# Unread products, a shared PSUM bank and a later start of heads and shared expert in the streamed stage of a transformer kernel

## The reference

```python
x = x + L0_attn(layernorm(x))       # ends in  a @ Wo + bo
x = x + L0_ffn(layernorm(x))        # router, routed experts, shared expert
x = x + L1_attn(layernorm(x))       # w_q_b, w_kv_b and w_o, 16 heads
x = x + L1_ffn(layernorm(x))

# in L0_ffn:
scores = softmax(x @ w_router.T); topw, topi = top_k(scores, 6)
routed = sum over the chosen experts of  topw * (silu(x @ g) * (x @ v) @ o)
out = routed + silu(x @ swg) * (x @ swv) @ swo
# in L1_attn:
w_o_abs = einsum('rhd,hde->hre', w_uv, w_o3)
q_abs   = einsum('bshd,rhd->bshr', q_nope, w_uk)
```

## Time and profile before

| | us |
|---|---|
| median of 3 runs | 2289.82 |
| lowest and highest | 2288.16, 2292.33 |
| the profiled execution, its time | 2300.19 |
| the profiled execution, its span | 2298.7 |
| the changed stage in the trace | 603 to 819 |
| idle of GpSimd before scatters, waiting for slots | 77.0 |

### The profile page before, as it was taken

One profiled execution on the slowest core, in us unless ns is written; L12 is line 12 of the kernel. 1 busy time (PEld: TensorE's weight loads), 2 busy tenths in 40 slices (PEclk: granted clock), 3 DMA queues, 4 the chain that ended last, 5 costly groups with the idle time before them and its releaser, 6 DMA issues. The chain is left out here.

```text
span 2298.7 us, 41540 instructions
## 1 busy us (share of the span) xinstructions
PE 1993.8 (87%) x11702; PEld 1336.9 (58%) x11766; DVE 1451.2 (63%) x3115; ACT 1256.6 (55%) x2558; POOL 882.9 (38%) x899
## 2 busy tenths in 40 slices
PE   4987999999767679999648899999698999996698
PEld 1552333333345469999624577777545777775587
DVE  4887888888355579999257566665265555543443
ACT  0793777777533147777114577777144777771322
POOL 1340000000054647797053277777001666670100
PEclk7896999999967889999869899999898999998899
DMA  7953000000531259898321012112000111012000
GB/s 210 289 104 56 2 0 0 1 0 1 126 118 59 83 168 267 263 287 266 106 69 41 10 45 53 42 42 56 14 0 1 24 24 35 21 35 68 1 19 19
DMA packets 185938, 173.83 MB, mean 76 GB/s; under 512 B 19651, under 2 KB 170741, under 8 KB 184822
## 3 DMA queue, kind: packets, MB, share of 16 engines
q1 hardware_dynamic: 173750, 143.23, 22.6%
q0 software_dynamic: 10720, 29.44, 3.9%
q10 hardware_dynamic: 1376, 0.02, 0.0%
HBM read 96.15 MB, written 61.60 MB: 69 GB/s over the span
## 5 line engine op out<-in xcount | busy, mean ns | idle before, releaser
L2638 POOL TENSOR_TENSOR w_rest<-work,w_head 128x512 fp32r<-128x512 f32 (+3 forms) x384 | 395.4, 1041 | 224.9 <-ACT w_head L2595 222.6
L790 DVE TENSOR_REDUCE half_max<-m_ps 128x1 f32<-128x512 f32 x512 | 317.2, 683 | 58.2 <-PE m_ps L712 57.6
L2484 DVE TENSOR_REDUCE piece_max<-m_ps 128x1 f32<-128x512 f32 (+3 forms) x384 | 201.1, 549 | 205.9 <-PE m_ps L2411 161.7
L847 ACT ACTIVATE weights<-s_ps 128x512 f32<-128x512 f32 x512 | 266.2, 601 | 108.2 <-PE s_ps L730 108.2
L2591 ACT ACTIVATE work<-s_ps 128x512 f32<-128x512 f32 (+3 forms) x384 | 187.4, 488 | 103.0 <-PE s_ps L2439 79.0
L2595 ACT ACTIVATE w_head<-work 128x512 fp32r<-128x512 f32 (+3 forms) x384 | 201.3, 524 | 56.9 <-PE o_ps L2448 46.7
L712 PE MATMUL m_ps<-kT,qT 96*128 (+1 forms) x512 | 204.3, 400 | 8.5 <-DVE half_max L790 6.6
L730 PE MATMUL s_ps<-qT,kT 99*128 (+1 forms) x512 | 193.3, 384 | 9.5 <-DMA qT<-max_rows 5.1
L2448 PE MATMUL o_ps<-w_head,lat_head 128*128 128x512 f32 (+3 forms) x384 | 184.4, 480 | 1.4 <-POOL w_rest L2638 1.4
L887 POOL COPY v_now<-v 128x83 f32 (+1 forms) x64 | 16.0, 256 | 366.6 <-PE o_ps L742 361.7
L1095 POOL TENSOR_TENSOR gv_rest<-ex_wgv,gv_head 128x736 fp32r<-128x736 f32 x64 | 113.9, 1779 | 75.8 <-ACT gv_head L1192 75.8
(11 more groups left out here) (395 smaller groups left out, 5050.8 us busy)
## 6 DMA issues: line engine op xcount, KB each, us to landing
slots<-zero SPq DMA_DIRECT2D x8, 3456.0 KB, 27.5
rows<-slots SPq DMA_DIRECT2D x64, 256.0 KB, 3.4
slots<-ex_out SPq DMA_DIRECT2D x64, 256.0 KB, 3.0
ex_wgv<-in_L_ffn_wg_dram SPq DMA_DIRECT2D x72, 176.0 KB, 3.0
ex_wgv<-in_L_ffn_wv_dram SPq DMA_DIRECT2D x72, 176.0 KB, 3.3
ex_wo<-in_L_ffn_wo_dram SPq DMA_DIRECT2D x72, 128.0 KB, 3.2
oT<-work SPq DMA_DIRECT2D x64, 128.0 KB
w_down<-l_inverse SPq DMA_DIRECT2D x32, 256.0 KB
```

The lines of the kernel that those rows point to most:

```text
L790: dve.tensor_reduce(half_max[:, u:u + 1], m_ps[:, BANK[u], :], AX.X, ALU.max).then_inc(max_done, 1)
L847: act.activation(w[:, s % 2 * 4 + j, :], s_ps[:, BANK[4 * s + j], :], ACT.Exp, scale=HD ** -0.5).then_inc(w_done, 1)
L2484: dve.tensor_reduce(piece_max[:, qt, k0 // 512:k0 // 512 + 1], m_ps[:, r % 2, 0:n], AX.X, ALU.max).then_inc(d["max_done"], 1)
L2638: pool.tensor_tensor(w_rest[:, s % 3, c0:512], w[:, s % 3, c0:512], w_head[:, s % 3, c0:512], ALU.subtract).then_inc(d["w_rest_done"], 1)
```

## The change

It has four parts. `keep_busy(n)` issues n matmuls of 128 x 512 in bf16 (identity by identity) into a bank of its own, `busy_ps`, which nobody reads; they wait for nothing and signal nothing. They stand before every `head` (2 before the second head of a pair, which is computed at the start of the next step, 1 before the first), before `shared_up` (1), before `ranks` (2), before `shared_down` (1), and 16 once before the first `turn_head`: 88 in all. The bank is won by putting the logits into the unused half of `x_ps`. For that, `logit(t)` waits until ScalarE has copied the turned rows of tile t + 1 in place of tile t, and `turn_x(t)` waits for the copy of the logits of tile t - 2. HEADS_AT goes from 6 to 7 and CHUNKS_AT from 14 to 15, on all engines, and STEPS with it from 23 to 24.

```diff
-    HEADS_AT, CHUNKS_AT = 6, 14
+    HEADS_AT, CHUNKS_AT = 7, 15
     STEPS = CHUNKS_AT + T // 2 + 1
...
-        l_ps = l.ps("l_ps", [P, 512])
+        busy_ps = l.ps("busy_ps", [P, 512])
...
+        l_ps = x_ps[:, D:D + NE]
...
+                def keep_busy(n):
+
+                    for _ in range(n):
+                        pe.matmul(busy_ps[:, :].rearrange("p (a b) -> p a b", a=4), c.identb[:, :],
+                                  c.identb[:, :].unsqueeze(1).to_broadcast([P, 4, P]), start=True, stop=True)
...
                 def turn_x(t):
                     pe.wait_ge(d["xn_done"], t + 1)
                     reuse(pe, d["x_copied"], t, 1)
+                    reuse(pe, d["log_copied"], t, 2)
...
-                    pe.wait_ge(d["x_copied"], t + 1)
+                    pe.wait_ge(d["x_copied"], min(t + 2, T))
                     reuse(pe, d["log_copied"], t, 1)
...
                     if 0 < h <= H1:
+                        keep_busy(2)
                         head(h - 1)
                     if 0 <= n < T // 2:
+                        keep_busy(1)
                         shared_up(n)
                     if 0 <= s - 2 < T:
                         turn_x(s - 2)
...
+                    if h == 0:
+                        keep_busy(16)
                     if 0 <= h < H1:
                         turn_head(h)
                     if 0 <= s - 3 < T:
                         logit(s - 3)
                     if 0 <= h < H1:
+                        keep_busy(1)
                         head(h)
                     if 0 <= s - 4 < T:
+                        keep_busy(2)
                         ranks(s - 4)
                     if 0 <= h < H1:
                         turn_head(h + 1)
                     if n > 0:
+                        keep_busy(1)
                         shared_down(n - 1, 0)
                         shared_down(n - 1, 1)
```

More of the change, by code:

```diff
@@ L1604, in logit @@
                         pe.wait_ge(d["wr_copied"], 1)
-                    pe.wait_ge(d["x_copied"], t + 1)
+                    pe.wait_ge(d["x_copied"], min(t + 2, T))
                     reuse(pe, d["log_copied"], t, 1)
                     for k in range(DK):
-                        i = pe.matmul(l_ps[:, 0:NE], xT[:, k, t * P:(t + 1) * P], w_r[:, k, :], start=k == 0,
+                        i = pe.matmul(l_ps, xT[:, k, t * P:(t + 1) * P], w_r[:, k, :], start=k == 0,
                                       stop=k == DK - 1)
@@ L1727, in copy_logits @@
                     act.wait_ge(d["log_done"], t + 1)
-                    act.activation(logits[:, t, :], l_ps[:, 0:NE], ACT.Copy).then_inc(d["log_copied"], 1)
+                    act.activation(logits[:, t, :], l_ps, ACT.Copy).then_inc(d["log_copied"], 1)
                 def deviation(t):
```

## The result

Over 20 runs of each, the changed kernel has a median of 2297.42 us (2290.67 to 2307.27) and the kernel before 2291.28 us (2282.01 to 2303.25): a ratio of 1.0027 with a 95% interval of [1.0015, 1.0039]. The change makes the kernel some 6 us slower, 3 to 9. The forecast was 6.6 us faster, and 2297.42 lies just outside the range's upper end of 2297.0.

A forecast was written before the change was run, and what follows sets the result against it. The streamed stage was taken as a chain round TensorE, ScalarE and VectorE per token tile, GpSimd's scatters at its end. Terms -4.5 - 6.1 + 3 + 1 = -6.6 us took 2289.82 to 2283.2 us, range 2268 to 2297.

The forecast's parts named there:

- The move: Heads and shared expert one step later: last slot earlier; -4.5 us, the middle of 0.75 and 8.25 us gain.
- The bank: Logits in the turned rows' bank wait for ScalarE's copy, 0.9 us in three shared steps, mostly covered: +1 us.
- The clock: Heads' stretch: products raise TensorE's mean clock from 0.74 to about 0.87; half of 16.3 us, times busy share: -6.1 us.
- given back: Rival: clock rises, but late signals stay and the gain becomes "remote" idle; 2289 us (2286 to 2292), chance 0.22.
- The products: The 88 unread matmuls on TensorE, mostly covered by idle time, leave some open before ranks and in shared steps: +3 us.
- The sixteen: Products before the first turned head, 3.7 to 6.9 us inside a 10.5 us wait for loads: costed at nothing.
- The slower rival: Clock in the heads' stretch stays at 0.74 or below, each product 0.43 us: +11 us, 2301 us, chance 0.16.
- Carrying the profile over: Whole kernel: the 10.4 us by which the median lay below the profiled execution was carried over unchanged.

The follow-up runs named there:

- e4: The changed kernel without its 88 unread products, move and shared bank kept: ratio 0.9992 to the kernel before, median 2288.21 us.
- e8: The changed kernel with unread products tripled everywhere but the sixteen, 232 in all: ratio 1.0057 to the kernel before, median 2307.90 us.
- e17: The changed kernel without the sixteen products before the first turned head, the other 72 kept: ratio 1.0002 to the kernel before, median 2295.47 us.
- e9: The changed kernel with only the sixteen products before the first turned head, move and bank kept: ratio 0.9987 to the kernel before, median 2294.71 us.
- e7: The changed kernel with each 512-column product cut into eight of 64 columns: ratio 1.0055 to the kernel before, median 2306.89 us.
- e1: The kernel before with only heads and shared expert moved by one step: ratio 0.9976 to the kernel before, median 2288.97 us.
- e16: The changed kernel with products cut into eighths and one scatter per tile in place of six: ratio 0.9772 to the kernel before, median 2237.77 us.

## Why the prediction was wrong

**The move (-4.5).** Right by itself: -5.5 [-8.9, -1.8]. The ranks of step 6 start at 630.63 in the changed kernel, before 636. But the last scatter came at 800.53, only 1.8 us before 802.33, with the first turned head 3.2 us earlier (638.87 against 642.11 in the earlier trace rows): in the changed kernel the gain of the move was spent before the last slot.

**The bank (+1).** Its run gives -0.7 [-4.6, 3.2]; the term is within it and too small to be told.

**The clock (-6.1).** This is the step that failed. The excess of cold time was there and a good part of it went (118.66 to about 102 us of other work, some 17, where I had 16.3 in the heads' stretch and 5.3 in the shared one as the most), though the mean in the heads' stretch came to 0.77 and not to 0.87. I then took TensorE's busy share, 68.85/92.1, as the share in which it is waited for. Beside the scatters the saved time did not reach the end of the stage (177.3 us in the changed kernel, 160.2 in e4, 174.6 in the kernel before): in the longest waits TensorE's results were there, and ScalarE took them up later (13.1 us in the longest case, 87.8 us of late waits in place of 77.7). The busy share did not measure who is waited for. This is the mechanism of the rival *given back*, and the sign that I gave for it, grown "remote" idle, is there (77.7 to 87.8 us); but I had put its end at 2289 us, since I let it only take the gain and not add to the loss. Between e4 and e8 the clock rose from 0.78 to 0.89 and the kernel became 15 us slower by the ratios. The Trainium skill, "TensorE: Matmul & The Clock Gate", section "Terms", reckons the penalty as the throttled time by one minus the clock's share; no such gain shows in these runs, but since each of them also added products, they don't test that rule by itself.

**The products (+3).** This term failed with it: the runs measure clock and products only together. Cover by idle time was the argument; the products did lie in the idle time, and the idle time before the heads still grew from 16.8 to 21.8 us. With signals on time, 88 products measured 2.5 to 5 us, near the forecast of 3, but the clock rose there too, from 0.94 to 1.00, and the figure is known to 7. Clock and products together I had at -3.1 us; measured are +8 with the move and +4 without, each known to 5. How much of it is late signals and how much the products' own time is not shown. The sixteen, costed at nothing, go with about 6 of these in e17 and with none in e9. The slower rival had 11 us for products that stay cold; its sign was right, but the clock rose, and the cost is as high with clock 0.84 and 0.89.

**Carrying the profile over.** The profiled execution of before was 9 us above the kernel's median, and I carried that over as a constant. The profiled time less the start of the last matmul is 1479 to 1491 us in all twenty profiles, 1483.5 in the kernel before, so an execution that is longer than another is longer mostly in this stage. The 77.7 us of late signals, the 0.74 and the 19.09 us of the earlier trace rows belong to a long execution; in e4's, 16 us shorter, there are 62.4 us. I had sized the clock's term and two rivals from a stage that was probably some 9 us longer than usual.

**What stays open.** What holds the signals, and in e7 TensorE itself: the runs show that both go on time when five of six scatters are gone, not whether GpSimd's issuing, the transfers or something else does it. How the 8 us share out over the places. And whether the late time is as large in an execution without the profiler; e1's profile is 14 us below the one of before, its ratio only 5.5 us.

The best of the kernels are the move alone (0.9976) and the move with the bank and the sixteen products of the shared expert (0.9967 [0.9945, 0.9989]); these two cannot be told apart, and both are faster than before and than the changed kernel.

## What to carry to other kernels

Before filling an engine's idle time to raise its clock, look at who releases the waits: if results stand finished while their reader idles, as here, a faster or busier producer may gain nothing, and its cold clock may be a consequence. Count what the filler costs its engine: here 25.6 us of products bought back 17. Test the cause by cutting the suspected neighbour (here five of six scatters, 56 us) before treating the symptom. And compare the profiled execution's time with the median, and ask in which stage the difference lies, before sizing terms from its waits.

## What the hardware did that I had not expected

- A copy that waits only for a matmul started 13.1 us after that matmul had ended (639.46 to 652.51), beside GpSimd's indirect DMAs of 0.97 us every 1.28 us until 650.07; with one scatter for a tile the same copy followed 0.6 us after it.
- Beside such DMAs TensorE did 60 matmuls of 64 columns, which wait for nothing, in 15.9 us (e7), and all 128 in 3.9 us with one scatter for a tile (e16).
- Taking scatters away raised TensorE's mean clock from 0.79 to 0.93 in an otherwise unchanged program, more than 88 or 232 products did (0.83, 0.89).
- 704 unread matmuls of 64 columns in place of 88 of 512 cost 9.5 us by the medians (6.4 by the ratios, known to 6) beside all scatters, and nothing that five runs can tell with one scatter for a tile.
